# Graph attention on one core: which engine ends a block of query rows, and where the count transposes stand among the scores

## The reference

```python
h = jnp.maximum(_layernorm(x, axis=-1), 0.0)
q = (h[src] @ qW).reshape(e, 4, 24); k = (h[dst] @ kW)...; v = (h[dst] @ vW)...
exp_s = jnp.exp(jnp.clip(jnp.einsum('ehd,ehd->eh', q, k), -10.0, 10.0))
norms = segment_sum(exp_s, src)[src]
res = segment_sum((exp_s / (norms + 1e-08))[:, :, None] * v, src)
x = x + h + res
```

## Time and profile before

| what | value |
|---|---|
| median of 3 runs | 1166.79 us (1166.59 to 1166.88) |
| span of the profiled execution | 1161.5 us |
| busy in it: PE, DVE, ACT, POOL | 1003.2, 876.5, 608.1, 492.1 us |
| attention, first scores to last add of x | 412.7 to 789.4 us |
| in the attention: PE, DVE, ACT, POOL busy | 366.5, 357.3, 334.8, 343.4 us |

### The profile page before, as it was taken

One profiled execution on the slowest core, in us unless ns is written; L12 is line 12 of the kernel. 1 busy time (PEld: TensorE's weight loads), 2 busy tenths in 40 slices (PEclk: granted clock), 3 DMA queues, 4 the chain that ended last, 5 costly groups with the idle time before them and its releaser, 6 DMA issues.

```text
span 1161.5 us, 23065 instructions
## 1 busy us (share of the span) xinstructions
PE 1003.2 (86%) x8302; PEld 612.5 (53%) x8302; DVE 876.5 (75%) x1318; ACT 608.1 (52%) x824; POOL 492.1 (42%) x522
## 2 busy tenths in 40 slices
PE   3887777777778779999999999996999699999995
PEld 2554455554544423223223333333669599999984
DVE  8668888888765569999999999997846654543366
ACT  7455556565563579898989898881100000001132
POOL 8434443343310069999999999980000000000000
PEclk9788999896897979999999999997999799999997
DMA  0010000000001631222222223221001100010111
GB/s 9 25 44 8 10 6 5 6 5 8 17 1 50 202 82 44 62 50 63 48 59 51 64 58 72 51 65 48 1 1 42 42 25 24 2 35 11 57 45 42
DMA packets 98715, 44.63 MB, mean 38 GB/s; under 512 B 85006, under 2 KB 96526, under 8 KB 98482
## 3 DMA queue, kind: packets, MB, share of 16 engines
q1 hardware_dynamic: 96914, 41.43, 13.4%
q0 software_dynamic: 1696, 1.74, 0.6%
HBM read 30.58 MB, written 12.56 MB: 37 GB/s over the span
## 4 chain that ended last, share of the span: by engine, by line
PE 77%; issue 9%; DVE 7%; ACT 3%; DMA 1%; POOL 1%; SPq 1%; DVEq 0%; ACTq 0%; POOLq 0%
PE PS L1298 18%; PE PS L1062 12%; PE PS L551 11%; PE PS L1072 11%; PE PS L555 8%; PE PS L1306 3%; PE PS L1773 3%; PE PS L1051 3%; ACT Eb L1114 2%; PE PS L1289 1%; POOL Eb L975 1%; DVE Eb L1134 1%; PE PS L875 1%; DMA kd<-QH 1%; PE PS L1759 1%
## 5 line engine op out<-in xcount | busy, mean ns | idle before, releaser
L1114 ACT ACTIVATE Eb<-PS,small 128x1024 f32<-128x1024 f32 (+4 forms) x350 | 333.3, 1003 | 45.0 <-PE PS L1062 40.3
L1134 DVE TENSOR_TENSOR Eb<-Eb,PS 128x2048 f32<-128x2048 f32 (+4 forms) x175 | 341.8, 2011 | 18.8 <-POOL Eb L975 10.1
L975 POOL TENSOR_SCALAR Eb<-Eb 128x1024 f32<-128x1024 f32 (+4 forms) x350 | 318.9, 935 | 76.7 <-ACT Eb L1114 73.2
L589 ACT ACTIVATE CT<-PS 128x500 f32 x313 | 183.7, 587 | 142.5 <-PE PS L555 134.3
L551 PE MATMUL PS<-mov,oneS 128*128 128x100 f16 x1565 | 183.3, 228 | 78.8 <-issue 74.7
L551 PEld LDWEIGHTS PS<-mov,oneS 128*128 128x128 f16 x1565 | 145.4, 105 | 158.4 <-issue 112.6
L1298 PE MATMUL PS<-hs,CT 128*128 128x192 f16 (+1 forms) x2500 | 213.3, 247 | 3.6 <-DVE SG L1539 1.6
L1298 PEld LDWEIGHTS PS<-hs,CT 128*128 128x128 f16 (+1 forms) x2500 | 207.9, 99 | 7.3 <-DVE SG L1539 2.3
L1062 PE MATMUL PS<-Qb,Kb 96*128 96x512 f16 (+3 forms) x700 | 180.4, 362 | 13.7 <-DMA Kb<-kd 10.8
L435 DVE TENSOR_TENSOR oneS<-iotaX,KL 128x2560 f16<-128x2560 int16 x80 | 120.4, 1505 | 70.3 <-PE PS L555 67.8
L1072 PE MATMUL PS<-Eb,V 128*25 128x512 f32 (+3 forms) x1400 | 166.7, 548 | 0.8 <-DVE Eb L1134 0.8
(11 more groups left out here) (281 smaller groups left out, 905.9 us busy)
## 6 DMA issues: line engine op xcount, KB each, us to landing
Kb<-kd SPq DMA_DIRECT2D x168, 96.0 KB, 2.3
qd<-QH SPq DMA_DIRECT2D x12, 192.0 KB, 2.7
kd<-QH SPq DMA_DIRECT2D x12, 192.0 KB, 3.1
hs<-t_d SPq DMA_DIRECT2D x12, 192.0 KB, 2.5
Qb<-qd SPq DMA_DIRECT2D x4, 384.0 KB, 3.8
CT<-x_d SPq DMA_DIRECT2D x1, 1200.0 KB, 7.1
x_d<-B SPq DMA_DIRECT2D x6, 192.0 KB, 1.9
t_d<-A SPq DMA_DIRECT2D x6, 192.0 KB, 1.8
```

What stands on the lines that cost most here:

```text
L589: a.activation(K.CT[:, :, bass.ds(words[g % 4][0], GI * W)], K.bank(g % 4)[:, 0:25 * GI * W].rearrange("p (a c) -> p a c", a=25), ACT.Copy ...
L975: g.tensor_scalar(e, e, EHI, ELO, ALU.min, ALU.max).then_inc(S("clamped"), 1)
L1114: a.activation(e, ps, ACT.Exp, scale=K.unsc[0:r, :]).then_inc(S("score_exp"), 1)
L1134: v.tensor_tensor(e, e, cn, ALU.mult).then_inc(S("weighed"), 1)
```

## The change

GpSimd adds x + h to a block's result, behind its clamps of the next block's tile 6 (and behind `gamma`, if there is one). ScalarE copies the sums from bank 4, before the exponentials of the next block's tile 3. VectorE keeps the division. TensorE transposes the counts between the two halves of the scores.

```diff
 def attn_gpsimd(g, K):
+    def add_x(b):
+        k = 4 * BN[b]
+        xv = K.xb[:, 0, 0:BN[b], :].rearrange("p t (h c) -> p (t h) c", c=24)
+        g.wait_ge(S("x1_new"), b + 1)
+        g.wait_ge(S("xb_in"), 16 * (b + 1))
+        g.tensor_tensor(xv, xv, K.accT[:, 0:k, :], ALU.add).then_inc(S("x1_sum"), 1)
...
         if it % FETCH == FETCH - 1 and it // FETCH < NT:
             gamma(g, K, it // FETCH)
+        if t == 6 and b:
+            add_x(b - 1)
+    add_x(6)
     g.wait_ge(S("clamped"), 2 * len(ITS))
+    g.wait_ge(S("x1_sum"), 7)
...
         if it + 2 < len(ITS):
             score(it + 2, 0)
-            score(it + 2, 1)
         if it + 1 < len(ITS):
             count(it + 1)
+        if it + 2 < len(ITS):
+            score(it + 2, 1)
         if it:
             value(it - 1)
...
 def attn_scalar(a, K):
+    def keep_sums(b):
+        wb = min(128 * BN[b], NP - 128 * B0[b])
+        a.wait_ge(S("valued"), 25 * b + 25)
+        if b:
+            a.wait_ge(S("sums_turned"), b)
+            a.wait_ge(S("x1_sum"), b)
+        a.activation(K.accS[:, 0:wb], K.bank(4)[:, 0:wb], ACT.Copy).then_inc(S("acc_free"), 1)
...
+        if t == 3 and b:
+            keep_sums(b - 1)
         for k in range(2):
...
+    keep_sums(6)
     a.wait_ge(S("score_exp"), 2 * len(ITS))
     a.activation(K.small[:, 140:141], K.identf[:, 0:1], ACT.Sqrt)
...
-    def keep_sums(b):
-        wb = min(128 * BN[b], NP - 128 * B0[b])
-        v.wait_ge(S("valued"), 25 * b + 25)
-        if b:
-            v.wait_ge(S("sums_turned"), b)
-            v.wait_ge(S("x1_sum"), b)
-        v.tensor_copy(K.accS[:, 0:wb], K.bank(4)[:, 0:wb]).then_inc(S("acc_free"), 1)
...
-        v.wait_ge(S("x1_new"), b + 1)
-        v.wait_ge(S("xb_in"), 16 * (b + 1))
-        v.tensor_tensor(xv, xv, K.accT[:, 0:k, :], ALU.add).then_inc(S("x1_sum"), 1)
 
     for it, (b, t) in enumerate(ITS):
         weigh(it)
-        if t == 0 and b:
-            keep_sums(b - 1)
         if t == 4 and b:
             add_result(b - 1)
-    keep_sums(6)
     add_result(6)
-    v.wait_ge(S("x1_sum"), 7)
+    v.wait_ge(S("x1_new"), 7)
```

More of the change, by code:

```diff
@@ L1152, in add_result @@
         v.wait_ge(step, own.n)
-        xv = K.xb[:, 0, 0:n, :].rearrange("p t (h c) -> p (t h) c", c=24)
         v.tensor_tensor(K.accT[:, 0:k, :], b7[:, :, 0:24], bcast_in(K.rec[:, 1, 0:k], k, 24), ALU.mult).then_inc(S("x1_new"), 1)
-        v.wait_ge(S("x1_new"), b + 1)
-        v.wait_ge(S("xb_in"), 16 * (b + 1))
-        v.tensor_tensor(xv, xv, K.accT[:, 0:k, :], ALU.add).then_inc(S("x1_sum"), 1)
     for it, (b, t) in enumerate(ITS):
         weigh(it)
-        if t == 0 and b:
-            keep_sums(b - 1)
         if t == 4 and b:
             add_result(b - 1)
-    keep_sums(6)
     add_result(6)
-    v.wait_ge(S("x1_sum"), 7)
+    v.wait_ge(S("x1_new"), 7)
 SRC_W = 20
```

## The result

The changed kernel takes 1170.39 us in the median of 13 runs (1164.35 to 1173.01), the kernel before 1166.76 us (1163.81 to 1169.49): a ratio of 1.0028, 95% interval 1.0015 to 1.0041. A second series of the same kernel gave 1168.60 us against 1167.21, ratio 1.0020 (1.0007 to 1.0033). It is slower by 0.2 to 0.3%; forecast was 1164.8 us, in a range of 1160.5 to 1169.0.

What follows compares the result with a forecast made beforehand. No engine alone bounds wide blocks, so waits between engines close the loop. Terms -1.0 - 2.7 + 0 + 1.2 + 0 + 0.5 give -2.0 us: 1164.8 us from 1166.8, range 1160.5 to 1169.

Steps and rivals of the forecast that it cites:

- Keys: Tile 9's key load queues behind the store awaiting GpSimd's add; chain 7.85 us wide, 6.9 block 4, 6.4 block 6.
- The add: GpSimd's add of x takes 1.0 us, 0.8 for 288 elements; bounds 0.46 and 1.72.
- Rival 2: GpSimd's add costs far more than 1 us, deciding from 1.35 us on: 1169 us, slower; chance 0.19.
- ScalarE's copy: Copy of the sums on ScalarE takes 0.65 us, delaying the next exponential and the scores after it; bounds 0.5 and 0.8.
- Block 6: 320 columns: tiles go to 1.57 us, 15 tiles, -1.3; keys +1.4; together 0.
- Blocks 1 to 3: Wide blocks take 57.8 us against 58.7, three times -0.9: -2.7 us.
- Block 0: The new order shrinks VectorE's waits after GpSimd's fetches: -1.0 us, bounds 0 and 2.2.
- Block 4: 384 columns: the wait for keys, up to 1.8 us, eats what the shorter tile gains: 0.
- block 5: A fetch in its tile 6 falls ahead of the add and lengthens the chain by 1.15 us: +1.2.
- the tail: VectorE's copy and add become ScalarE's copy and GpSimd's add, each handed over by a semaphore: +0.5 us.
- Rival 1: Tile 9's keys come in time; wide blocks gain 1.7 us each: -6.9, 1160 us; chance 0.17.
- Rival 3: The new order gives nothing: VectorE's lateness passes through the count to the scores, using up 1.3 us spare; 1167 us; chance 0.14.

Runs made afterwards that it cites:

- store_late: The changed kernel with the store of the sums moved from tile 5 to tile 7 in SyncE's list: 1162.65 us, ratio 0.9960.
- nk4: The changed kernel with a fourth buffer of keys (NK = 4), the store still in tile 5: 1161.66 us, ratio 0.9951.
- count_only: The kernel before with only the new order of the count transposes: 1165.96 us, ratio 0.9991.
- add_only: The kernel before with only the add of x moved to GpSimd: 1172.34 us, ratio 1.0048.
- late_wide: store_late with the new transpose order in wide blocks 0 to 3 only, the old one in blocks 4 to 6: 1160.92 us, ratio 0.9949.
- late_wide_no_add: late_wide with the add of x on VectorE again: 1162.59 us, ratio 0.9972.
- add_tile7: The changed kernel with GpSimd's add one tile later, behind the clamps of tile 7, the store unmoved: 1192.40 us in one run.
- copy_only: The kernel before with only the copy of the sums moved to ScalarE: 1164.10 us, ratio 0.9978.

## Why the prediction was wrong

- **Keys (right).** TensorE stands for tile 9's keys in every block, 1.16 us in block 1 (forecast 1.25), 1.02 and 0.50 in blocks 2 and 3, 2.53 in block 5 (about 3). The chains of 7.85, 6.9 and 6.4 us came out within 0.1 us in blocks 1, 4 and 6. store_late and nk4 take the stand away and gain 6 us. The wait and its place were forecast; that the change as a whole loses by it was not.
- **The add (right).** 0.99 us in the median for 1.0; 0.79 to 0.81 for 288 elements. Rival 2 is out. The Trainium skill (GPSIMD Engine Reference, section 3.1), by the estimate in the prediction, gave 0.84; the row decides for 1.0:

```profile
L976 POOL TENSOR_TENSOR xb<-xb,accS x7: 790/991/1013, 491.2 to 793.8; 128x384 f32<-128x384 f32 x4, 128x288 f32<-128x288 f32 x3
```

- **ScalarE's copy (right in kind).** 0.60 us for 0.65, without a table load. Behind a stand for keys it gives nothing back, which the forecast did not see.
- **Block 6 (the step that failed).** "tiles alternate between 1.75 and 1.56 us and go to 1.57: 15 tiles, -1.3". I took the count off the chain between ScalarE and TensorE and compared with TensorE's own tile of the old order. But the new order makes TensorE's own tile longer, 1.67 us: the gap of 0.27 us between scores and transposes becomes 0.37 between scores and value sums. In place of -1.3 the order costs +0.84 (count_only). The keys cost +1.25 (add_only) for +1.4. Together +2.1 for 0: more than half of the 3.9 us between -2.0 and +1.9. Without these 2.1 us the attention would by the sum be 0.2 us shorter than before, and not 1.9 longer.
- **Blocks 1 to 3 (a size).** -1.8 for -2.7: block 2 takes 8.5 us from tile 6's to tile 9's scores, where I had one chain of 7.85 for all three. Its load takes 0.6 us longer to land than the 2.43 us in that sum allow.
- **Block 0 (a size).** -0.5 for -1.0. Over all profiles the orders differ by 0.1 to 1.8 us there, but most of that is the half clock at the block's start; the two profiles compared here have the same clock there, 0.69. So half of the forecast came.
- **Block 4, block 5, the tail (right).** +0.2 for 0, +1.35 for +1.2, +0.55 for +0.5. In block 5 there is luck in it: the clock stayed at 1.00 behind the stand of 2.53 us, and where it fell behind one of 2.52 (add_only) the block was 3.0 us longer than before.
- **The rivals.** Rival 1 is out by the stand. Rival 3's mechanism, VectorE's lateness passing through the count to the scores, is there in blocks 2 and 3 of the changed kernel (0.70 and 0.40 us between the halves of tile 8's scores), where the prediction had 1.3 us to spare; the stand for keys behind it hides it. With the keys in time it counts: in late_wide's block 2 the same 0.70 us stand, and the step to tile 9's scores is 3.06 us and not 2.20. Its worst case is block 1 of late_wide_no_add. A rival was missing: that the new order itself costs TensorE time.
- **The range.** The attention's error of 3.9 us alone gives 1168.7, within it; the second series (1168.60) is too, the first is not. Two terms were put at nothing: the 0.45 us that the move of the add costs outside the span, and the stages outside the attention, which spread over 4 us and had no share of the range. The distance of 5.3 us between span and median, which the prediction kept, did no harm, as the sum starts from the median; the runs show 2.0, so the profiled execution was a quick one.

## What to carry to other kernels

When an operation moves to another engine, follow its semaphore into every queue that waits for it: here a store in a list of loads, nearly harmless behind the old engine (0.3 us), cost 6 us behind the new one, and moving it by two tiles turned a loss of 0.3% into a gain of 0.4%. Before taking an instruction off a cross-engine chain by reordering, price the new succession on its own engine: an engine's time for a tile belongs to an order, not to a set of instructions. A gain of one part can vanish or grow beside another (the copy: -2.1 us alone, 0 beside the add; the order: -0.2 alone and -4.2 beside both, of which some 2.4 go with the clock), so the parts are best run apart and together, and compared block by block.

## What was not expected of the hardware

- A wait of TensorE can cost twice, but need not. Behind the stand of 3.13 us in add_tile7 the granted clock is 0.57 over 7 us; behind its 2.71 us in block 3 and the 2.53 us of the changed kernel's block 5 it stayed at 1.00, and behind 2.52 us in add_only's block 5 it was 0.76 over 7 us. At half clock two score matmuls take 1.01 us in place of 0.59. The Trainium skill (TensorE: Matmul & The Clock Gate, "Part 1: The HAM clock gate") says that half rate is the default, which recent activity lifts; the traces agree with the two levels.
- Value sums with 25 columns of fp32 weights start 0.37 us after a pair of 320-column score matmuls, transposes 0.27 us after it.
- VectorE's add of two SBUF operands, 288 elements wide, took 0.46 us at the tail, where GpSimd clamps nothing, and 1.11 us beside clamps in block 5 of the kernel before. Of 384 elements it took 0.96 to 1.08 us beside clamps there, and 1.75 in block 1 of late_wide_no_add. The same kind of collision can fall on GpSimd instead: in copy_only an add of 288 elements overlaps a clamp, takes 0.46 us all the same, and the clamp takes 1.12 us in place of 0.83. GpSimd's own add of 288 elements takes 0.8 us.
